# Finer waits for the gated products and the second feed-forward product of a fused adaLN and ternary feed-forward kernel

## Chip, core and metric

The kernel runs on one core of a Trainium2 chip. The metric is the time of one execution on the device, in microseconds (us). Before the change the median of 3 runs is 344.57 us (344.53 to 345.72). Differences of some 0.5% are about the smallest that can be told from no change here.

## What is computed

32 sequences of 32 tokens with 256 features go through a conditioned transformer layer and then through a gated feed-forward layer with ternary weights; the sum with the input is the result.

```python
def cond(x, timestep_embed, ...):                 # first layer
    shift1, scale1, gate1, shift2, scale2, gate2 = split(timestep_embed @ ada_w + ada_b, 6)
    x1 = ln(x) * (1 + scale1) + shift1
    q, k, v = (x1 @ qkv_w + qkv_b)                # 16 heads of 128
    a = softmax(q @ k.T * 128 ** -0.5) @ v        # inside each sequence of 32
    x = x + gate1 * (a @ out_w + out_b)
    x2 = ln(x) * (1 + scale2) + shift2
    h = gelu(x2 @ ffn_w1 + ffn_b1)                # 1024 wide
    return x + gate2 * (h @ ffn_w2 + ffn_b2)

def ffn(x, w1, g1, w2, g2, w3, g3):               # second layer, ternary weights, inputs quantised to int8
    swish = silu(linear_bit(x, w1, g1))           # 1024 wide
    h = swish * linear_bit(x, w2, g2)
    return linear_bit(h, w3, g3)

out = x + ffn(cond(x, cond_2048))
```

## The kernel before

Every engine's program is written out by hand as one list, and semaphores alone order the engines. The 1024 tokens are four quarters of 256 (`Q`, `b` or `a` in the code), and a quarter is two tiles `t` of 128 tokens. The 16 heads are four groups of four. A unit `u` is one group of heads over one quarter; there are 16 units. The products in float32 are made in three passes (`three_pass`): every operand is split into a high part and a low part, and high by high, high by low and low by high are added up in one bank of PSUM.

Units 0 to 7 do two groups of heads for all quarters. Then the loop over `q` (0 to 3) does the other two groups, two units for each `q`, and weaves in the feed-forward work that is ready: for quarter `b = q - 1` the first and second product of the first layer's feed-forward (`ffn1`, `ffn2`), for quarter `a = q - 2` the second layer. Behind the loop stands an ending, written out in one piece, with the rest of quarters 2 and 3. The change touches two kinds of work on TensorE (PE).

**The gated products** (`z_product`). For tile `t` and half `c` of the 1024 hidden columns, four matmuls of 128x512 are made: two (k = 0, 1) with w1 into bank 0 of a pair of banks, then two with w2 into bank 1. ScalarE (ACT) reads bank 0 and makes the swish (`silu`, semaphore `silu_done`). Then VectorE (DVE) reads bank 1 and the swish and multiplies them (`hidden`, semaphore `h_ready`). In the loop all four products of a quarter, (t, c) = (0,0), (0,1), (1,0), (1,1), use one pair, `wide_bank`, so each of the last three waits until `hidden` of the one before it has read bank 1. PE has other work between them: an output projection ahead of (0,1), and one head's query and key projection (`qk_unit`, two groups of six matmuls of 128x256) ahead of (1,0) and of (1,1). A further such head, the transposes `x2_turn` and another head follow, and then the value projection `v_unit`, which waits for `qk_kept`, ACT's copies of queries and keys. ACT's list has here: `silu` (1,1), the load of the exponential's table, the exponential, and only then those copies. The loop does this for quarters 0 and 1 (q = 2 and 3). In the ending, `end_z(0)` to `end_z(7)` do quarters 2 and 3 over three pairs of banks in turn, and from `end_z(3)` on a pair comes round again.

**The second product** (`ffn2`). ACT makes the hidden activations in four chunks of two tiles (`gelu`), and rounds each chunk to its high part `h_hi` (`h_high`, semaphore `h_hi_made`). GpSimd (POOL), or DVE for some, makes the low part `h_lo`. The first call of a quarter, `ffn2(b, 0)`, waits for all four high chunks. Its 24 matmuls are 8 with high by high, 8 with the weight's low part by `h_hi`, and 8 with `h_lo`, before which it waits for the low parts. It is called for quarters 0, 1 and 2; quarter 3 has its own form, `end_ffn2`, which the change leaves alone.

Of the kernel before, what the change touches and what calls it, by code (L numbers as in the profile page):

```python
# [60 lines left out]
def adaln_bitffn(nc, x, cond, ada_w, ada_b, qkv_w, qkv_b, out_w, out_b, ffn_w1, ffn_b1, ffn_w2, ffn_b2,  # L61
# [12 lines left out]
    MT = MLP // P  # L74
# [3 lines left out]
    NQ = T // QT  # L78
# [7 lines left out]
    NU = 2 * HALF  # L86
# [27 lines left out]
    with ExitStack() as ctx:  # L114
# [3 lines left out]
        def sem(name):  # L118
            return ctx.enter_context(nc.semaphore(name))
# [133 lines left out]
        proj_bank, att_bank, wide_bank = [[pair[:, i, :] for i in range(2)] for pair in (proj_banks, att_banks, wide_banks)]  # L253
# [17 lines left out]
        end_z_banks = [(proj_bank, att_bank, wide_bank)[i % 3] for i in range(len(END_Z))]  # L271
# [72 lines left out]
        at_lo_made = sem("at_lo_made")  # L344
# [16 lines left out]
        gelu_done = sem("gelu_done")  # L361
        h_hi_made = sem("h_hi_made")
        h_lo_made = sem("h_lo_made")
        h_lo_dve = sem("h_lo_dve")
        ffn2_mm = sem("ffn2_mm")
# [14 lines left out]
        silu_done = sem("silu_done")  # L380
        h_ready = sem("h_ready")
# [15 lines left out]
        out_ready = sem("out_ready")  # L397
# [147 lines left out]

        @block.tensor
        def _(pe):
            def three_pass(dst, pairs, start=True, stop=True, late=None):
                hi = [(a, c) for a, b, c, d in pairs]
                left_lo = [(b, c) for a, b, c, d in pairs]  # L550
                right_lo = [(a, d) for a, b, c, d in pairs]
                seq = hi + (left_lo + right_lo if late is not None and late[0] == "rhs" else right_lo + left_lo)
                for i, (l, r) in enumerate(seq):
                    if late is not None and i == 2 * len(pairs):
                        for made, n in late[1:]:
                            pe.wait_ge(made, n)
                    mm = pe.matmul(dst, l, r, start=start and i == 0, stop=stop and i == len(seq) - 1)  # L557
                return mm

            def qk_unit(u, h, late=None):  # L560
                g, Q, c, r = group(u), quarter(u), h // (HG // HALVES), h % (HG // HALVES)
                hi, lo = w_hi[g % 2], w_lo[g % 2]
                if r == 0:
                    pe.wait_ge(qk_hi, HALVES * g + c + 1)
                    pe.wait_ge(qk_lo, HALVES * g + c + 1)
                if h >= 2:
                    pe.wait_ge(qk_kept, 2 * HG * u + 2 * (h - 1))
                elif u > 0 and h == 0:
                    pe.wait_ge(shifted, u)
                elif u > 0:  # L570
                    pe.wait_ge(v_kept, 2 * u)
                for s in range(2):
                    cols = [slice(c * CH + (s * KD + k) * HW + r * P, c * CH + (s * KD + k) * HW + (r + 1) * P)
                            for k in range(KD)]
                    mm = three_pass(proj_bank[h % 2][:, s * QT:(s + 1) * QT],
                                    [(hi[:, cols[k]], lo[:, cols[k]], x1_hi[:, Q, k, :], x1_lo[:, Q, k, :])
                                     for k in range(KD)], late=late if s == 0 else None)
                mm.then_inc(projected, 1)
# [21 lines left out]
            def v_unit(u, t):  # L600
                g, Q = group(u), quarter(u)
                if t == 0:
                    pe.wait_ge(vw_hi, g + 1)
                    pe.wait_ge(vw_lo, g + 1)
                pe.wait_ge(qk_kept, 2 * HG * u + 2 * HG - 2 + 2 * t)
                tok = slice(t * P, (t + 1) * P)
                cols = [slice(SLOT + k * GC, SLOT + (k + 1) * GC) for k in range(KD)]
                three_pass(proj_bank[t][:, :],
                           [(x1_hi[:, Q, k, tok], x1_lo[:, Q, k, tok], w_hi[g % 2][:, cols[k]], w_lo[g % 2][:, cols[k]])
                            for k in range(KD)]).then_inc(projected, 1)  # L610
# [43 lines left out]
            def out_proj(u, t):  # L654
                g, Q, j = group(u), quarter(u), u % 2
                if t == 0:
                    pe.wait_ge(wo_hi_made, g + 1)
                    pe.wait_ge(wo_lo_made, g + 1)
                    if j == 0 and 0 < u <= HALF:
                        pe.wait_ge(acc_kept, u // 2)  # L660
                    elif j == 0 and u > HALF:
                        pe.wait_ge(out_read, Q)
                pe.wait_ge(at_hi_made, 2 * u + 2)
                three_pass(out_bank[:, t * D:(t + 1) * D],
                           [(at_hi[:, t, h, :], at_lo[:, t, h, :], wo_hi[g % 2][:, h, :], wo_lo[g % 2][:, h, :])
                            for h in range(HG)], start=(j == 0 and t == 0), stop=(j == 1 and t == 1),
                           late=("lhsT", (at_lo_made, 2 * u + 2)) if t == 0 else None).then_inc(out_mm, 1)
# [97 lines left out]
            def ffn2(b, t):  # L765
                if t == 0:
                    pe.wait_ge(f2_lo_made, 2)
                    pe.wait_ge(x2_scaled, b + 1)
                    pe.wait_ge(h_hi_made, (MT // 2) * (b + 1))
                    if b >= 1:  # L770
                        pe.wait_ge(hq_kept, 2 * b if b == NQ - 2 else 2 * b - 1)
                tok = slice(t * P, (t + 1) * P)
                lows = ((h_lo_made, (MT // 2) * (b + 1) - 2), (h_lo_dve, 2)) if b == NQ - 2 else (
                    (h_lo_made, (MT // 2) * (b + 1)),)
                three_pass(turn_bank[:, t * D:(t + 1) * D],
                           [(h_hi[:, m, tok], h_lo[:, m, tok], f2_hi[:, m, :], f2_lo[:, m, :])
                            for m in range(MT)],
                           late=("lhsT", *lows) if t == 0 else None).then_inc(ffn2_mm, 1)

            def end_ffn2(b, j):  # L780
                last = MT // 2 - 1
# [27 lines left out]
                                          rounded(xg[:, t, i, k * P:(k + 1) * P]), ident_h[:, :])  # L809
                mm.then_inc(q_turned, 1)  # L810

            def z_product(b, t, c, banks=wide_bank):
                if c == 0:
                    pe.wait_ge(q_kept, 2 * b + t + 1)
                if b < NQ - 2 and 2 * t + c > 0:
                    pe.wait_ge(h_ready, 4 * b + 2 * t + c)
                for i in range(2):
                    for k in range(KD):
                        mm = pe.matmul(banks[i][:, :], qt_bf[:, b, t, i * KD + k, :], w12t[:, i, k, c * MC:(c + 1) * MC],  # L819
                                       start=(k == 0), stop=(k == KD - 1))  # L820
                mm.then_inc(z_mm, 1)

            def end_z(i):
                b, t, c = END_Z[i]
                earlier = [j for j in range(i) if end_z_banks[j] is end_z_banks[i]]
                if earlier:
                    pe.wait_ge(h_ready, 4 * (NQ - 2) + earlier[-1] + 1)
                elif end_z_banks[i] is wide_bank:
                    pe.wait_ge(out_ready, 2 * (NQ - 2))
                elif end_z_banks[i] is att_bank:  # L830
                    pe.wait_ge(gelu_done, MT * NQ)
                else:
                    pe.wait_ge(at_lo_made, 2 * NU)
                z_product(b, t, c, end_z_banks[i])

            def hq_turn(b, t, rows, bank=turn_bank):
                pe.wait_ge(hq_rounded, 2 * b + t + 1)
# [75 lines left out]
            for q in range(NQ):  # L913
                u, b, a = HALF + 2 * q, q - 1, q - 2
# [10 lines left out]
                if a >= 0:  # L925
                    pe.wait_ge(at_lo_made, 2 * u)
                    z_product(a, 0, 0)
                    q_turn(a, 1)
                    score(u)
                out_proj(u - 1, 1)  # L930
                if a >= 0:
                    z_product(a, 0, 1)
# [17 lines left out]
                if u < NU - 1:  # L950
                    if b >= 0:
                        pe.wait_ge(at_lo_made, 2 * u)
                        ffn1(b, range(MT))
                    if a >= 0:
                        hq_turn(a, 0, h_tiles[0])
                    out_proj(u - 1, 1)
                    if a >= 0:
                        last_of_pair(a, b, 0)
                        hq_turn(a, 1, h_tiles[1], att_bank[0])
                    if b >= 0:  # L960
                        ffn2(b, 0)
                    if a >= 0:
                        last_of_pair(a, b, 1)
                    if b >= 0:
                        ffn2(b, 1)
# [3 lines left out]
            a, b = NQ - 2, NQ - 1  # L969
# [13 lines left out]
            for t in range(2):  # L983
                end_x2_turn(b, t)
            ffn2(a, 0)
            ffn2(a, 1)
            ffn1(b, range(MT), end_ffn1_bank, True)
# [1128 lines left out]
```

## Time and profile before

| | |
|---|---|
| median of 3 runs | 344.57 us |
| the profiled execution | 345.1 us |
| its span, first to last instruction | 343.3 us |
| PE busy | 333.1 us, 97% of the span |
| VectorE busy | 214.4 us, 62% |
| ScalarE busy | 182.3 us, 53% |
| GpSimd busy | 122.5 us, 36% |
| TensorE clock granted | 1.00 of full speed throughout |

The profile is one execution. The 1.8 us between its time and its span lie outside the instructions. The ends of matmuls are modelled, so two matmul rows overlap on the page, and the distance from one start to the next is what a matmul costs. An idle time in brackets counts from that modelled end. A row "x8" is a run of eight alike instructions with the start of the first.

### The profile page before, as it was taken

Reading aid. Unit: us, or ns where it says so; the run is one execution under the profiler, and the core shown is the slowest. Engines: PE = TensorE matmul, PEld = TensorE weight load, DVE = VectorE, ACT = ScalarE, POOL = GpSimd, SP = SyncE. Lnnn points to the kernel's source line nnn. Section 1 sums busy time; section 2 is a strip of 40 time slices with the busy share of each in tenths; the row PEclk is TensorE's granted clock in tenths of the full one; section 3 lists DMA queues with packets and bytes.
Section 4 is the critical chain, followed back from the end, with each engine's and each line's share of the span. In section 5 each row is a group of like instructions: output and inputs, shape, how many; then the busy total and the mean of one; then the engine's idle time right before and its main releaser. Section 6 shows DMA issues by size and latency. Waiting matters only on the chain. (4 is left out here: it accounts for less than half of the span.)

```text
span 343.3 us, 9835 instructions
## 1 busy us (share of the span) xinstructions
PE 333.1 (97%) x4205; PEld 301.2 (88%) x4205; DVE 214.4 (62%) x420; ACT 182.3 (53%) x352; POOL 122.5 (36%) x112
## 2 busy tenths in 40 slices
PE   8999999999999999999999999999999999999886
PEld 8889989899998989989898998789998789997665
DVE  3647966825859942513376064689375599865886
ACT  2654554455424565356334535478263667437684
POOL 2364405001923861656020630225330233113681
DMA  7974930500063540210020000200010200100001
GB/s 243 365 266 150 316 130 0 154 2 2 2 205 106 179 149 13 63 32 2 2 64 4 1 32 0 63 3 2 26 37 2 63 3 2 64 31 2 0 2 61
DMA packets 20834, 24.41 MB, mean 71 GB/s; under 512 B 1780, under 2 KB 18328, under 8 KB 20792
## 3 DMA queue, kind: packets, MB, share of 16 engines
q1 hardware_dynamic: 20416, 23.50, 21.1%
q8 instruction: 33, 0.54, 0.6%
q10 hardware_dynamic: 376, 0.30, 0.3%
q14 instruction: 9, 0.07, 0.1%
HBM read 22.68 MB, written 1.11 MB: 69 GB/s over the span
## 5 line engine op out<-in xcount | busy, mean ns | idle before, releaser
L1605 ACT ACTIVATE q_t<-proj_banks,bias_cols 128x256 f32<-128x256 f32 x64 | 30.5, 477 | 55.5 <-PE proj_banks L557 55.5
L557 PE MATMUL proj_banks<-x_hi,w_hi 128*128 128x256 f32 x252 | 52.8, 291 | 0.0
L557 PE MATMUL proj_banks<-x_lo,w_hi 128*128 128x256 f32 x252 | 50.7, 283 | 0.0
L557 PE MATMUL proj_banks<-x_hi,w_lo 128*128 128x256 f32 x252 | 50.7, 283 | 0.0
L1198 DVE TENSOR_TENSOR v_sb<-proj_banks,bv_row 128x512 f32<-128x512 f32 x32 | 21.7, 685 | 31.5 <-PE wide_banks L650 30.0
L557 PEld LDWEIGHTS proj_banks<-x_hi,w_hi 128*128 128x128 f32 x252 | 39.6, 191 | 1.5 <-issue 0.6
L557 PEld LDWEIGHTS proj_banks<-x_hi,w_lo 128*128 128x128 f32 x252 | 39.2, 191 | 0.0
L557 PEld LDWEIGHTS proj_banks<-x_lo,w_hi 128*128 128x128 f32 x252 | 39.2, 191 | 0.0
L650 PEld LDWEIGHTS att_banks<-probs_t,v_sb 32*128 32x128 f32 x512 | 29.8, 186 | 5.5 <-issue 5.4
L650 PE MATMUL att_banks<-probs_t,v_sb 32*128 32x32 f32 x512 | 31.6, 272 | 0.0
L1605 ACT ACTIVATE k_t<-proj_banks,bias_cols 128x256 f32<-128x256 f32 x64 | 30.2, 471 | 0.0
L650 PE MATMUL wide_banks<-probs_t,v_sb 32*128 32x32 f32 x480 | 29.6, 272 | 0.0
L650 PEld LDWEIGHTS wide_banks<-probs_t,v_sb 32*128 32x128 f32 x480 | 27.9, 186 | 0.0
L1614 ACT CAST at_hi<-att_banks 128x512 fp32r<-128x512 f32 x16 | 9.4, 588 | 33.0 <-PE wide_banks L650 32.6
L2000 POOL TENSOR_TENSOR h_lo<-work,h_hi 128x512 fp32r<-128x512 f32 x10 | 15.1, 1523 | 21.3 <-ACT h_hi L1692 21.0
L557 PE MATMUL proj_banks<-w_hi,x_hi 128*128 128x512 f32 x64 | 22.1, 427 | 0.4 <-ACT k_t L1605 0.4
L1941 POOL TENSOR_TENSOR w_lo<-stage,w_hi 128x1024 fp32r<-128x1024 f32 x6 | 15.2, 2547 | 18.6 <-DVE w_hi L1153 15.0
L557 PE MATMUL out_bank<-wo_hi,at_hi 128*128 128x256 f32 x128 | 21.8, 292 | 0.0
L557 PE MATMUL out_bank<-wo_hi,at_lo 128*128 128x256 f32 x128 | 20.3, 280 | 0.0
L557 PE MATMUL out_bank<-wo_lo,at_hi 128*128 128x256 f32 x128 | 20.3, 280 | 0.0
L557 PE MATMUL proj_banks<-w_lo,x_hi 128*128 128x512 f32 x64 | 20.0, 393 | 0.0
L557 PE MATMUL proj_banks<-w_hi,x_lo 128*128 128x512 f32 x64 | 19.9, 392 | 0.0
(299 smaller groups left out, 774.3 us busy)
## 6 DMA issues: line engine op xcount, KB each, us to landing
stage<-in_L_cond_qkv_w SPq DMA_DIRECT2D x16, 256.0 KB, 4.5
gate<-gate_rows_scratch SPq DMA_DIRECT2D x48, 64.0 KB, 2.4
stage<-in_L_cond_qkv_w SPq DMA_DIRECT2D x4, 512.0 KB, 5.3
stage<-in_L_cond_out_w SPq DMA_DIRECT2D x4, 512.0 KB, 4.4
work<-in_L_ffn_w SPq DMA_DIRECT2D x2, 1024.0 KB, 9.7
xin<-in_x SPq DMA_DIRECT2D x7, 256.0 KB, 2.9
bv_row<-in_L_cond_qkv_b SPq DMA_DIRECT2D x4, 256.0 KB, 5.0
work<-in_L_cond_ada_w SPq DMA_DIRECT2D x1, 1024.0 KB, 10.3
```

The costliest lines, as they stand in the source:

```text
L557: mm = pe.matmul(dst, l, r, start=start and i == 0, stop=stop and i == len(seq) - 1)
L650: mm = pe.matmul(dst, v_sb[r, t, h * P:(h + 1) * P], probs_t[r, t * HG + h, :], start=True, stop=True)
L1198: dve.tensor_tensor(v_sb[:, t, :], proj_bank[t][:, :], bv_row[:, u % 2, :], ALU.add).then_inc(v_kept, 1)
L1605: act.activation(dst[:, h, :], proj_bank[h % 2][:, s * QT:(s + 1) * QT], ACT.Identity, bias=bias_cols[:, c:c + 1]).then_inc(qk_kept, 1)
L1614: act.copy(att_to(at_hi, p), att_from(u, p)).then_inc(at_hi_made, 1)
L1941: pool.tensor_tensor(w_lo[g % 2][:, s], stage[:, s], w_hi[g % 2][:, s].bitcast(F32), ALU.subtract).then_inc(qk_lo, 1)
L2000: pool.tensor_tensor(h_lo[:, m, :], hf(2 * j, 2), h_hi[:, m, :].bitcast(F32), ALU.subtract).then_inc(h_lo_made, 1)
```

## The change

`z_product` now waits for two things at two places. Ahead of its two matmuls into bank 0 it waits for the swish of the product that used the pair before (`silu_done`), and ahead of the two into bank 1 for that product's gating (`h_ready`). Before, one wait for `h_ready` stood ahead of all four. `end_z` passes the number on instead of waiting itself, for the products from the fourth on. `ffn2(b, 0)` waits for the high parts chunk by chunk: one chunk ahead of each pair of its first eight matmuls, instead of all four chunks ahead of the first.

```diff
-            def three_pass(dst, pairs, start=True, stop=True, late=None):
+            def three_pass(dst, pairs, start=True, stop=True, late=None, each=None):
...
                 for i, (l, r) in enumerate(seq):
+                    if each is not None and i < len(pairs) and i % 2 == 0:
+                        pe.wait_ge(each[0], each[1] + i // 2 + 1)
...
                     pe.wait_ge(x2_scaled, b + 1)
-                    pe.wait_ge(h_hi_made, (MT // 2) * (b + 1))
...
-                           late=("lhsT", *lows) if t == 0 else None).then_inc(ffn2_mm, 1)
+                           late=("lhsT", *lows) if t == 0 else None,
+                           each=(h_hi_made, (MT // 2) * b) if t == 0 else None).then_inc(ffn2_mm, 1)
...
-            def z_product(b, t, c, banks=wide_bank):
+
+            def z_product(b, t, c, banks=wide_bank, held=None):
                 if c == 0:
                     pe.wait_ge(q_kept, 2 * b + t + 1)
                 if b < NQ - 2 and 2 * t + c > 0:
-                    pe.wait_ge(h_ready, 4 * b + 2 * t + c)
+                    held = 4 * b + 2 * t + c
                 for i in range(2):
+                    if held is not None:
+                        pe.wait_ge((silu_done, h_ready)[i], held)
...
-                if earlier:
-                    pe.wait_ge(h_ready, 4 * (NQ - 2) + earlier[-1] + 1)
-                elif end_z_banks[i] is wide_bank:
-                    pe.wait_ge(out_ready, 2 * (NQ - 2))
-                elif end_z_banks[i] is att_bank:
-                    pe.wait_ge(gelu_done, MT * NQ)
-                else:
-                    pe.wait_ge(at_lo_made, 2 * NU)
-                z_product(b, t, c, end_z_banks[i])
+                held = 4 * (NQ - 2) + earlier[-1] + 1 if earlier else None
+                if not earlier:
...
+                z_product(b, t, c, end_z_banks[i], held)
```

PE's list at product (1,0) of a quarter in the loop, before; its rows name the bank's pair, the operands and, in brackets, the semaphores waited for:

```order
L557 MATMUL proj_banks<-x_hi,w_lo_62 128x256 x2
L819 MATMUL wide_banks<-w12t,qt_bf 128x512 [waits h_ready,q_kept]
L819 MATMUL wide_banks<-w12t,qt_bf 128x512 x3
L557 MATMUL proj_banks<-x_hi,w_hi_60 128x256 [waits v_kept]
L557 MATMUL proj_banks<-x_hi,w_hi_60 128x256
```

The wait for `h_ready` held all four matmuls, and the next head's projection behind them. PE's list at the same place after:

```order
L559 MATMUL proj_banks<-x_hi,w_lo_62 128x256 x2
L824 MATMUL wide_banks<-w12t,qt_bf 128x512 [waits silu_done,q_kept]
L824 MATMUL wide_banks<-w12t,qt_bf 128x512
L824 MATMUL wide_banks<-w12t,qt_bf 128x512 [waits h_ready]
L824 MATMUL wide_banks<-w12t,qt_bf 128x512
L559 MATMUL proj_banks<-x_hi,w_hi_60 128x256 [waits v_kept]
L559 MATMUL proj_banks<-x_hi,w_hi_60 128x256
```

The wait for `h_ready` now stands two matmuls later; the matmuls and their order are the same. PE's list at `ffn2(0, 0)`, before, with the end of an output projection ahead of it:

```order
L557 MATMUL out_bank<-wo_hi_63,at_lo 128x256 x4
L557 MATMUL turn_bank<-f_hi,h_hi 128x256 [waits h_hi_made,x2_scaled,f2_lo_made]
L557 MATMUL turn_bank<-f_hi,h_hi 128x256 x7
L557 MATMUL turn_bank<-f_lo,h_hi 128x256 x8
L557 MATMUL turn_bank<-f_hi,h_lo 128x256 [waits h_lo_made]
L557 MATMUL turn_bank<-f_hi,h_lo 128x256 x7
```

One wait for all four chunks stood at its head. The same place after:

```order
L559 MATMUL out_bank<-wo_hi_63,at_lo 128x256 x4
L559 MATMUL turn_bank<-f_hi,h_hi 128x256 [waits h_hi_made,x2_scaled,f2_lo_made]
L559 MATMUL turn_bank<-f_hi,h_hi 128x256
L559 MATMUL turn_bank<-f_hi,h_hi 128x256 [waits h_hi_made]
L559 MATMUL turn_bank<-f_hi,h_hi 128x256
...
L559 MATMUL turn_bank<-f_lo,h_hi 128x256 x8
L559 MATMUL turn_bank<-f_hi,h_lo 128x256 [waits h_lo_made]
```

The row with its own wait and the one behind it stand there three times, once for each further chunk, so the wait for the last chunk moved behind six matmuls. No other engine's list changes.

## Rows read from the trace of the kernel before

**Rows 1.** The page, first part: engine, busy us, share of the span, instructions

```profile
PE 333.1 (97%) x4205; PEld 301.2 (88%) x4205; DVE 214.4 (62%) x420; ACT 182.3 (53%) x352; POOL 122.5 (36%) x112
```

**Rows 2.** Waits of PE, longest first: total us, times, longest us

```profile
PE wide_banks L819 <- DVE work L1363: 0.7, 2, 0.4
...
PE wide_banks L819 <- DVE h_odd L1363: 0.5, 2, 0.3
```

**Rows 3.** Timeline (start us, us long, engine), PE, products (1,0) and (1,1), quarter 0

```profile
217.80 0.40 PE L557 MATMUL proj_banks<-x_hi,w_lo 128*128 128x256 f32 x2
218.58 1.02 PE L819 MATMUL wide_banks<-w12t,qt_bf 128*128 128x512 fp8e4 x4 [0.38 <-DVE work L1363]
219.25 0.59 PE L557 MATMUL proj_banks<-x_hi,w_hi 128*128 128x256 f32 x2
...
220.63 0.40 PE L557 MATMUL proj_banks<-x_hi,w_lo 128*128 128x256 f32 x2
221.29 1.04 PE L819 MATMUL wide_banks<-w12t,qt_bf 128*128 128x512 fp8e4 x4 [0.26 <-DVE h_odd L1363]
```

**Rows 4.** Timeline of ACT (swishes) and of DVE (gatings) around these products

```profile
216.88 0.69 ACT L1719 ACTIVATE work<-wide_banks,deq 128x512 f32<-128x512 f32 x1 [2.24 <-PE wide_banks L819]
...
219.69 0.69 ACT L1719 ACTIVATE work<-wide_banks,deq 128x512 f32<-128x512 f32 x1 [0.61 <-issue]
...
217.68 0.75 DVE L1363 SCALAR_TENSOR_TENSOR work<-wide_banks,deq,work 128x512 f32<-128x512 f32 x1 [0.27 <-ACT work L1719]
...
220.48 0.75 DVE L1363 SCALAR_TENSOR_TENSOR h_odd<-wide_banks,deq,work 128x512 f32<-128x512 f32 x1 [1.17 <-ACT work L1719]
```

**Rows 5.** Timeline: PE's product (0,0) of quarter 0, which finds its banks free

```profile
212.33 1.04 PE L819 MATMUL wide_banks<-w12t,qt_bf 128*128 128x512 fp8e4 x4
213.20 0.39 PE L808 MATMUL turn_bank<-ident_h,work 128*128 128x128 f16 x4
```

**Rows 6.** Timeline: ACT's last copy ahead of the value projection, and that projection

```profile
225.19 0.46 ACT L1605 ACTIVATE k_t<-proj_banks,bias_cols 128x256 f32<-128x256 f32 x1
...
225.79 0.70 PE L557 MATMUL proj_banks<-w_hi,x_hi 128*128 128x512 f32 x2 [0.18 <-ACT k_t L1605]
```

**Rows 7.** Timeline of PE, ACT and POOL at `ffn2(0, 0)`

```profile
193.21 0.63 PE L557 MATMUL out_bank<-wo_hi,at_lo 128*128 128x256 f32 x4
194.22 1.19 PE L557 MATMUL turn_bank<-f_hi,h_hi 128*128 128x256 f32 x8 [0.38 <-ACT h_hi L1692]
...
196.20 1.12 PE L557 MATMUL turn_bank<-f_hi,h_lo 128*128 128x256 f32 x8
...
193.46 0.62 ACT L1692 CAST h_hi<-work 128x512 fp32r<-128x512 f32 x1
...
194.15 1.29 POOL L2000 TENSOR_TENSOR h_lo<-work,h_hi 128x512 fp32r<-128x512 f32 x1
```

**Rows 8.** Timeline at `ffn2(2, 0)`, and at four like transposes of quarter 0

```profile
223.59 0.60 PE L734 MATMUL turn_bank<-ident,xt 128*128 128x128 f32 x4
223.95 0.48 PE L557 MATMUL proj_banks<-x_hi,w_hi 128*128 128x256 f32 x2
...
297.40 0.60 PE L742 MATMUL att_banks<-ident,xt 128*128 128x128 f32 x4
298.00 1.18 PE L557 MATMUL turn_bank<-f_hi,h_hi 128*128 128x256 f32 x8
...
297.12 0.62 ACT L1692 CAST h_hi<-work 128x512 fp32r<-128x512 f32 x1
```

**Rows 9.** Timeline: PE at the head of `ffn1`'s seventh tile, which has a wait

```profile
237.34 0.40 PE L557 MATMUL wide_banks<-x_hi,f_lo 128*128 128x256 f32 x2
237.58 0.40 PE L557 MATMUL wide_banks<-x_hi,f_hi 128*128 128x256 f32 x2
```

**Rows 10.** Timeline: the last gated product (`end_z(7)`), and ACT's seventh swish

```profile
328.51 1.04 PE L819 MATMUL att_banks<-w12t,qt_bf 128*128 128x512 fp8e4 x4
...
329.39 0.68 ACT L1729 ACTIVATE late_swish<-proj_banks,deq 128x512 f32<-128x512 f32 x1
```

More of the change, by code:

```diff
@@ L825, in end_z @@
                 earlier = [j for j in range(i) if end_z_banks[j] is end_z_banks[i]]
-                if earlier:
-                    pe.wait_ge(h_ready, 4 * (NQ - 2) + earlier[-1] + 1)
-                elif end_z_banks[i] is wide_bank:
-                    pe.wait_ge(out_ready, 2 * (NQ - 2))
-                elif end_z_banks[i] is att_bank:
-                    pe.wait_ge(gelu_done, MT * NQ)
-                else:
-                    pe.wait_ge(at_lo_made, 2 * NU)
-                z_product(b, t, c, end_z_banks[i])
+                held = 4 * (NQ - 2) + earlier[-1] + 1 if earlier else None
+                if not earlier:
+                    if end_z_banks[i] is wide_bank:
+                        pe.wait_ge(out_ready, 2 * (NQ - 2))
+                    elif end_z_banks[i] is att_bank:
+                        pe.wait_ge(gelu_done, MT * NQ)
+                    else:
+                        pe.wait_ge(at_lo_made, 2 * NU)
+                z_product(b, t, c, end_z_banks[i], held)
             def hq_turn(b, t, rows, bank=turn_bank):
```

## The prediction

> **What bounds the kernel now.** I read the busy times of the page first. PE is busy for 333.1 us, 97% of the span, and VectorE, the next, for 62% [rows 1]. So until the ending, time comes only from PE's idle gaps, and an edit that removes no matmul, like this one, can give back at most the gaps it touches. The second view is the list of PE's waits. In the loop it names DVE's gating as releaser of the gated products four times, 0.7 us in two and 0.5 us in two [rows 2]. Six products have the changed wait there, three for each of two quarters, so two of them, (0,1) of each quarter, show no gap. The third view is the timeline around these gaps and around the three calls of `ffn2(b, 0)`. Idle times in brackets count from a modelled end; I work from starts instead: a row's start plus its number of matmuls times their cost is when PE could have gone on.
>
> **Costs used.** A gated product of four matmuls takes 213.20 - 212.33 = 0.87 us [rows 5], so a pair takes 0.43. Two matmuls of 128x256 take 237.58 - 237.34 = 0.24 us [rows 9].
>
> **Product (1,0).** PE is ready at 217.80 + 0.24 = 218.04 and starts at 218.58 [rows 3], 0.54 late. The swish that reads bank 0 ends at 216.88 + 0.69 = 217.57 [rows 4], before PE is ready, so the pair into bank 0 can start at 218.04 and is done at 218.47. The gating that reads bank 1 ends at 217.68 + 0.75 = 218.43 [rows 4], and PE went on 0.15 behind that. So the pair into bank 1 starts at 218.58, as the whole product did, and ends at 219.01 instead of 219.44. Gain: 0.43 us, the pair that now lies inside the wait. DVE still ends last here; 0.11 us of the gap stays.
>
> **Product (1,1).** All that leads to it follows the first by 0.43 us. The next swish started at 219.69, that is 1.11 behind the start of the first product's matmuls and 0.25 behind the end of the last; it becomes 219.26. Its gating started 0.79 later and took 0.75 [rows 4]; it becomes 220.05 to 220.80. PE is ready at 220.63 + 0.24 - 0.43 = 220.44 and the swish ends at 219.95, so bank 0's pair runs from 220.44 to 220.87. Bank 1 is read by 220.80. Between that end and PE's start lay 221.29 - 221.23 = 0.06 here [rows 3, 4], so PE may go on at 220.86 and finds its queue ready at 220.87. The product ends at 221.30 instead of 221.29 + 0.87 = 222.16: 0.86 us in all. The margin is 0.01 us, but a miss costs only its own size.
>
> **What comes next, and whether it follows.** The next place at which PE stands is the value projection, at 225.79, behind ACT's copy that ends at 225.19 + 0.46 = 225.65 [rows 6]. If that copy kept its time, the gain would be lost. ACT's list ahead of it is the swish of (1,1), a table load, the exponential and the copies, without a pause, and that swish starts when product (1,1) ends. So the copy moves by the same 0.86 us. Gain of a quarter: 0.86 us. The same pair of gaps stands in quarter 1 (two waits in each of the two rows) [rows 2], and the neighbouring work is the same: 2 x 0.86 = 1.72 us.
>
> **`ffn2(0, 0)`.** PE is ready at 193.21 + 0.48 = 193.69 and starts at 194.22 [rows 7], 0.53 late, because the fourth high chunk ends at 193.46 + 0.62 = 194.08. The three chunks before it are long made. Six matmuls on them take 0.72 us, until 194.41, and by then (194.22) the fourth chunk may be read. So the gap goes entirely: 0.53 us. What is late next? The low parts: POOL's last one ends at 194.15 + 1.29 = 195.44, and PE used it at 196.20 [rows 7]. Now PE comes at 195.67. With 0.14 us from an engine's end to PE's start, as for the high chunk, that still holds, by 0.09 us.
>
> **`ffn2(1, 0)` and `ffn2(2, 0)`.** The first has no wait of PE behind `h_hi` in the list, so nothing. For the second, four transposes precede it at 297.40; four like ones took 223.95 - 223.59 = 0.36 [rows 8], so PE was ready at 297.76 and started at 298.00. The last chunk ended at 297.12 + 0.62 = 297.74 [rows 8]. Gain at most 0.24 us; at least zero, if the transposes themselves waited for their input and PE was ready later than that. I take 0.22, near the upper end, since the 0.60 us that these four span is what the like ones span.
>
> **The ending.** `end_z(3)` to `end_z(7)` get the finer wait. Only the last shows a gap for it. It could start about 0.1 us earlier than 328.51, but ACT's list decides there: the swish of `end_z(6)` only starts at 329.39 [rows 10], so the last swish has to queue behind it. Nothing.
>
> **Cost of the waits themselves.** The change adds 20 waits on PE: 6 in the loop's products, 5 in the ending's, 9 in `ffn2`. A wait whose semaphore is already up shows no cost: `ffn1`'s seventh tile has one, and its first pair starts 0.24 us after the pair before, as everywhere [rows 9]. I take zero. The upper bound is in the third rival. The Trainium skill (Perfetto Trace Analysis, Identifying Dependency Chains) says that an instruction that waits on several engines may get separate EventSemaphore instructions ahead of it. That speaks against product (1,0), whose head waits for ACT's copy and ACT's swish; no row of this trace shows a price for it, and with none the sum stays as it is.
>
> **Sum.** 1.72 + 0.53 + 0.22 = 2.47 us. Everything behind these places is fed by PE or by what PE releases, so the ending should move as one block. The profiled execution would go from 345.1 to 342.6 us. Its own time lies 0.5 us above the median, 344.57; against that the forecast is 344.57 - 2.47 = **342.1 us**, 0.7% faster.
>
> **Rivals.**
> *Part of the gain is absorbed.* Product (1,1) needs swish and gating to move with (1,0), and the value projection needs ACT's copies to move too. If ACT or DVE is held by something PE doesn't feed (POOL's norm for DVE's next step, say), (1,0) still gives 0.43 and (1,1) nothing lasting: 2 x 0.43 + 0.53 = 1.4 us, giving 343.2. Against it: ACT sat idle for 0.61 us ahead of the swish of (1,0) and DVE for 1.17 us ahead of its gating [rows 4].
> *The change does nothing.* A PE wait that goes away reappears wholly at the next place fed from another engine, the value projection [rows 6] or, for `ffn2`, POOL's low part [rows 7]: 344.5 us. Against it: I found each of those feeders to start from the very product that moved.
> *Slower.* A wait in the middle of a product keeps the next weight load from running ahead under the matmuls before it. If each such load were exposed, by about 0.24 us (as much as a pair of 128x256 matmuls), 20 waits would cost 4.8 us against 2.47 gained: 346.9. It decides from 2.47 / 20 = 0.12 us for each. Its place is between the bank 0 and bank 1 pairs. The Trainium skill (TensorE: Matmul & The Clock Gate, on the reorder window) says that PE's queue pulls weight loads ahead of matmuls in flight, which is what such a wait would forbid. Against it stand the 0.24 us at the satisfied wait [rows 9].
> *More than forecast.* If the small gap left at (1,0) closes as well, and work behind gets a kinder overlap between DVE and POOL, 3.0 us: 341.5.
>
> **How the numbers follow.** Forecast 0.64, part absorbed 0.18, nothing 0.08, slower 0.04, more 0.06. The forecast's own range is 341.8 to 342.7, that is 1.9 to 2.8 us gained. The range to hold 8 in 10 takes in most of the absorbed case: 341.5 to 343.3. About 0.5%, 1.7 us, is what a measurement of this kernel can tell from no change; that bound lies at 342.85. Faster by more: 0.64 + 0.06 + a little of the absorbed case = 0.73. Slower by more: 0.03. Within: 0.24.
>
> **What the profile after would show.** Product (1,0): its row splits in two, with bank 0's pair right behind the projection and 0.1 us of gap before bank 1's pair. Product (1,1): no gap. The list of PE's waits has lost `wide_banks <- DVE`, or nearly. `ffn2(0, 0)` starts without a gap and its low-part matmuls wait for nothing. The value projection still waits 0.18 us for ACT's copy. The distance from `ffn2(0, 0)`'s end to the start of `ffn2(2, 0)` is 1.7 us shorter. I am wrong if new waits stand at the value projection or at POOL's low part, if a pair's spacing at a new wait is over 0.24 us where the semaphore is up, or if the ending, from the last feed-forward product on, is longer than before.

## The result and the profile after

The kernel after takes 342.18 us (median of 5 runs, 341.83 to 342.30), the kernel before 344.53 us (median of 5). The ratio is 0.9925, with a 95% interval of 0.9913 to 0.9936: 0.75% faster, where 0.7% was forecast (342.1 us, range 341.5 to 343.3). A second set of runs of the kernel after, on another occasion, gave 341.78 us and a ratio of 0.9905 (0.9878 to 0.9932).

The page's first part after, to be read beside [rows 1]; the profiled execution takes 342.06 us and its span is 340.3 us:

```profile
PE 331.5 (97%) x4205; PEld 300.1 (88%) x4205; DVE 214.4 (63%) x420; ACT 182.2 (54%) x352; POOL 122.5 (36%) x112
```

The work is the same to the instruction. The whole list of PE's waits after:

```profile
PE out_bank L810 <- DVE work L1346: 1.2, 1, 1.2
PE att_banks L868 <- DVE probs_t L1079: 1.0, 1, 1.0
PE proj_banks L559 <- ACT k_t L1610: 0.6, 3, 0.3
PE turn_bank L1026 <- issue: 0.6, 1, 0.6
PE wide_banks L1026 <- ACT late_hw L1902: 0.6, 1, 0.6
PE proj_banks L589 <- DVE xt L1146: 0.5, 1, 0.5
PE out_bank L559 <- DVE h_lo L1544: 0.4, 1, 0.4
PE att_banks L858 <- ACT late_hqt L1748: 0.4, 1, 0.4
PE att_banks L824 <- ACT qt_bf L1715: 0.2, 1, 0.2
```

The rows of [rows 2], `wide_banks` behind DVE's gating, are gone, and so is a wait of `turn_bank` behind `h_hi`. Of the three waits for `k_t` two are those of the value projections; the third, 0.3 us, lies in the first 14 us of the program and is looked at below. PE's timeline after at products (1,0) and (1,1) of quarter 0 and at the value projection behind them, to be read beside [rows 3] and [rows 6]; the last line is ACT's copy ahead of that projection:

```profile
216.93 0.40 PE L559 MATMUL proj_banks<-x_hi,w_lo 128*128 128x256 f32 x2
217.17 1.05 PE L824 MATMUL wide_banks<-w12t,qt_bf 128*128 128x512 fp8e4 x4
217.87 0.59 PE L559 MATMUL proj_banks<-x_hi,w_hi 128*128 128x256 f32 x2
...
219.24 0.40 PE L559 MATMUL proj_banks<-x_hi,w_lo 128*128 128x256 f32 x2
219.49 1.04 PE L824 MATMUL wide_banks<-w12t,qt_bf 128*128 128x512 fp8e4 x4
...
223.99 0.70 PE L559 MATMUL proj_banks<-w_hi,x_hi 128*128 128x512 f32 x2 [0.18 <-ACT k_t L1610]
...
223.38 0.47 ACT L1610 ACTIVATE k_t<-proj_banks,bias_cols 128x256 f32<-128x256 f32 x1
```

The product starts 0.24 us behind the row before it, the cost of two matmuls, where it was 0.78 us (218.58 - 217.80). At (1,1) it is 0.25 us, where it was 0.66. Each is one row of four matmuls: there is no gap between the two banks' pairs either. The value projection has the same 0.18 us of idle time as before and starts 4.50 us behind product (1,1), as before: ACT's copies have moved with the product.

Here is what holds bank 1's pair now. PE's weight load for it and DVE's gating ahead of it, after:

```profile
217.61 0.11 PEld L824 LDWEIGHTS wide_banks<-w12t,qt_bf 128*128 128x128 bf16 x2 [0.33 <-DVE work L1368]
...
216.81 0.75 DVE L1368 SCALAR_TENSOR_TENSOR work<-wide_banks,deq,work 128x512 f32<-128x512 f32 x1 [0.27 <-ACT work L1724]
...
219.10 0.75 DVE L1368 SCALAR_TENSOR_TENSOR h_odd<-wide_banks,deq,work 128x512 f32<-128x512 f32 x1 [0.66 <-ACT work L1724]
```

The gating ends at 216.81 + 0.75 = 217.56, the weight load starts 0.05 us behind it, and bank 0's pair keeps PE at work until 217.17 + 0.43 = 217.60. So the wait for the gating now lies under bank 0's pair, and only the weight loads' row shows it.

PE at `ffn2(0, 0)` and at `ffn2(2, 0)` after, beside [rows 7] and [rows 8]; the last line is POOL's last low part for `ffn2(0, 0)`:

```profile
192.93 0.63 PE L559 MATMUL out_bank<-wo_hi,at_lo 128*128 128x256 f32 x4
193.40 1.12 PE L559 MATMUL turn_bank<-f_hi,h_hi 128*128 128x256 f32 x8
...
195.32 1.12 PE L559 MATMUL turn_bank<-f_hi,h_lo 128*128 128x256 f32 x8
...
294.68 0.60 PE L744 MATMUL att_banks<-ident,xt 128*128 128x128 f32 x4
295.05 0.71 PE L559 MATMUL turn_bank<-f_hi,h_hi 128*128 128x256 f32 x4
...
193.88 1.29 POOL L2005 TENSOR_TENSOR h_lo<-work,h_hi 128x512 fp32r<-128x512 f32 x1
```

The product starts 0.47 us behind the projection row (1.01 before) and 0.37 us behind the transposes (0.60 before). Its low part follows at 1.92 us, without the 0.06 us by which it was slower before (1.98).

**A measure that does not depend on the head of the program.** The first changed instruction comes some 193 us into the span. Ahead of it the kernels have the same instructions, and yet the output projection row ahead of `ffn2(0, 0)` starts at 193.21 us in the profile of before [rows 7] and at 192.93 after. Over the eight profiles here with the same instructions up to there it lies between 192.51 and 193.21. So two spans can differ by 0.7 us for a reason that no edit has. The difference arises in the first 14 us. PE's first product with the layer's input `xt`, before and then after, and in the profile of after a wait behind it:

```profile
10.03 1.99 PE L587 MATMUL proj_banks<-xt,stage 128*128 128x256 f32 x8 [0.52 <-DVE xt L1141]
```

```profile
9.42 1.99 PE L589 MATMUL proj_banks<-xt,stage 128*128 128x256 f32 x8 [0.53 <-DVE xt L1146]
...
13.13 0.47 PE L559 MATMUL proj_banks<-x_hi,w_hi 128*128 128x256 f32 x2 [0.29 <-ACT k_t L1610]
```

In the eight profiles this product starts between 9.40 and 10.05 us, and from its start to the output projection it is 183.09 to 183.18 us in seven of them. In the profile of after it is 183.51, and that one alone has the wait at 13.13 us. The second profile of after does not have it, so it is not an effect of the change. Below I take the distance from the start of that row to the start of the last product's row of matmuls. The last rows, before and then after:

```profile
339.54 1.04 PE L1043 MATMUL turn_bank<-w3t,late_hqt 128*128 128x256 fp8e4 x8
```

```profile
336.51 1.04 PE L1048 MATMUL turn_bank<-w3t,late_hqt 128*128 128x256 fp8e4 x8
```

Before: 339.54 - 193.21 = 146.33 us. After: 336.51 - 192.93 = 143.58 us, 2.75 less. The second profile of after gives 143.55: the two differ by 0.03 us.

### The profile page after: what moved, and what is told of

It reads as the page before. It is cut to its first block and busy times, and to the rows that moved or that the text cites. A ratio compares the mean times of both kernels' runs of the same rounds, so it can differ in the third digit from the quotient of the medians.

```text
span 340.3 us, 9835 instructions
## 1 busy us (share of the span) xinstructions
PE 331.5 (97%) x4205; PEld 300.1 (88%) x4205; DVE 214.4 (63%) x420; ACT 182.2 (54%) x352; POOL 122.5 (36%) x112
```

## Experiments

The ratios of the experiments are to runs of the kernel before on the same chip as each experiment (there were three chips), whose medians were 344.86 to 344.94 us. Two distances are read from each profile: `tail`, the one just defined, and `gated`, from the start of product (0,0) to the start of the value projection, for quarters 0 and 1.

| kernel | tail us | gated us | median us | ratio to before, 95% interval |
|---|---|---|---|---|
| before | 146.33 | 13.46, 13.45 | 344.53 | |
| after | 143.58 | 12.53, 12.53 | 342.18 | 0.9925 (0.9913 to 0.9936) |
| e1_chunks | 145.56 | 13.46, 13.45 | 343.69 | 0.9966 (0.9952 to 0.9979) |
| e2_split_loop | 144.49 | 12.54, 12.53 | 342.92 | 0.9952 (0.9938 to 0.9965) |
| e3_split_end | 146.25 | 13.46, 13.45 | 344.43 | 0.9983 (0.9961 to 1.0004) |
| e4_swap | 146.18 | 13.39, 13.38 | 344.44 | 0.9993 (0.9984 to 1.0003) |
| e5_one_wait | 143.58 | 12.54, 12.55 | 341.64 | 0.9900 (0.9886 to 0.9915) |
| e6_two_waits | 145.33 | 12.59, 12.52 | 346.07 | 1.0033 (1.0020 to 1.0046) |
| e8_separate | 143.83 | 12.68, 12.66 | 342.15 | 0.9916 (0.9902 to 0.9931) |
| e7_order | 143.02 | 12.38, 12.39 | 341.00 | 0.9884 (0.9867 to 0.9900) |
| e9_order_before | 145.13 | 12.99, 13.01 | 343.72 | 0.9967 (0.9948 to 0.9986) |
| e10_after | 143.55 | 12.54, 12.52 | 341.78 | 0.9905 (0.9878 to 0.9932) |

By their times, e3_split_end and e4_swap can't be told from the kernel before. What is said of them rests on the distances of one profile each.

### Each part alone

e1_chunks is the kernel before with the chunked wait of `ffn2(b, 0)` alone:

```diff
+                    if each is not None and i < len(pairs) and i % 2 == 0:
+                        pe.wait_ge(each[0], each[1] + i // 2 + 1)
...
-                    pe.wait_ge(h_hi_made, (MT // 2) * (b + 1))
```

> The kernel before with one part of the change alone: ffn2(b, 0) waits for the high parts chunk by chunk. Theory (the gaps add up, and what is gained is kept to the end): the gap at ffn2(0, 0) goes, 0.54 us, and 0.23 us at ffn2(2, 0), together 0.77 us; the time goes from 344.5 to 343.8 us, and the distance from ffn2(0, 0)'s start to the last matmul changes by 0.23 us alone. Rival (absorbed): the gain reappears as a longer wait for POOL's low part or at the value projection, and the distances behind grow by what was gained; 344.5 us.

```profile
192.83 0.63 PE L559 MATMUL out_bank<-wo_hi,at_lo 128*128 128x256 f32 x4
193.30 1.12 PE L559 MATMUL turn_bank<-f_hi,h_hi 128*128 128x256 f32 x8
...
296.49 0.60 PE L744 MATMUL att_banks<-ident,xt 128*128 128x128 f32 x4
```

These are PE's rows of e1_chunks. The product starts 0.47 us behind the projection (1.01 before), and `tail` is 146.33 - 145.56 = 0.77 us shorter. `gated` is what it was. The rival, that POOL's low part or the value projection takes the gain, has fallen.

e2_split_loop is the kernel before with the split wait for the six products in the loop alone:

```diff
-                if b < NQ - 2 and 2 * t + c > 0:
-                    pe.wait_ge(h_ready, 4 * b + 2 * t + c)
+                held = 4 * b + 2 * t + c if b < NQ - 2 and 2 * t + c > 0 else None
                 for i in range(2):
+                    if held is not None:
+                        pe.wait_ge((silu_done, h_ready)[i], held)
```

> The kernel before with the finer wait of the gated products in the loop alone (six products of quarters 0 and 1). Theory: product (1,0) starts 0.54 us earlier and (1,1) another 0.43 us, in each of two quarters, 1.9 us in all: 344.5 becomes 342.6 us, with the distance from product (0,0) to the next value projection 12.53 instead of 13.46 us in both quarters. The recorded prediction's own size for it was 1.72 us: 342.8. Rival (absorbed): (1,0) alone keeps its gain, 0.9 to 1.1 us: 343.5.

`gated` fell by 0.92 us in both quarters and `tail` by 1.84 us. The three matmul rows of e2_split_loop that matter, products (0,0), (1,0) and (1,1), with the value projection:

```profile
211.72 1.04 PE L820 MATMUL wide_banks<-w12t,qt_bf 128*128 128x512 fp8e4 x4
...
217.44 1.05 PE L820 MATMUL wide_banks<-w12t,qt_bf 128*128 128x512 fp8e4 x4
219.75 1.04 PE L820 MATMUL wide_banks<-w12t,qt_bf 128*128 128x512 fp8e4 x4
224.26 0.47 PE L557 MATMUL proj_banks<-w_hi,x_hi 128*128 128x512 f32 x1 [0.17 <-ACT k_t L1606]
```

From (0,0) to (1,0) it is 5.72 us (218.58 - 212.33 = 6.25 before), and from (1,0) to (1,1) 2.31 us (2.71 before). Both gains are kept; absorption would have shown as a `gated` near 12.9.

e3_split_end is the kernel before with the split for `end_z(3)` to `end_z(7)` alone:

```diff
+                held = 4 * (NQ - 2) + earlier[-1] + 1 if earlier else None
...
-                    pe.wait_ge(h_ready, 4 * (NQ - 2) + earlier[-1] + 1)
...
+                z_product(b, t, c, end_z_banks[i], held)
```

> The kernel before with the finer wait in end_z(3) to end_z(7) alone. Theory: no time from the bank 0 wait itself, since ACT's list decides the ending. The waits at the head of end_z(4) change their places, though: the one for ACT's copy is now the one carried by the matmul and no longer a separate wait instruction, and PE starts 0.06 instead of 0.14 us behind that copy. So 0.08 us off the ending, 344.45 us. Rival (a gap is a gap): the 0.12 us ahead of end_z(7) come off the end too, 0.2 us in all; or nothing changes at all.

PE's row of `end_z(4)` before, and then PE's and ACT's rows of e3_split_end in the ending:

```profile
325.79 1.02 PE L819 MATMUL att_banks<-w12t,qt_bf 128*128 128x512 fp8e4 x4 [0.30 <-ACT qt_bf L1710]
```

```profile
325.00 1.04 PE L824 MATMUL att_banks<-w12t,qt_bf 128*128 128x512 fp8e4 x4 [0.21 <-ACT qt_bf L1715]
...
327.60 1.03 PE L824 MATMUL att_banks<-w12t,qt_bf 128*128 128x512 fp8e4 x4
...
324.84 0.59 ACT L1715 ACTIVATE qt_bf<-turn_bank 128x512 bf16<-128x512 f16 x1
...
328.61 0.68 ACT L1734 ACTIVATE late_swish<-proj_banks,deq 128x512 f32<-128x512 f32 x1
```

`end_z(4)` at 325.00 starts 0.62 us behind the transposes ahead of it; it was 0.70. `end_z(7)` at 327.60 comes 2.60 us behind `end_z(4)`, where it was 2.72: its gap of 0.12 us has gone. But ACT's swish of `end_z(6)` starts 1.01 us behind `end_z(7)`'s start, and no longer 0.88 (329.39 - 328.51, [rows 10]). From `end_z(4)` to that swish it is 3.61 us, and it was 3.60. The 0.12 us are given back there. Of the ending 0.08 us remain in `tail`, as was expected; the rival with 0.2 us has fallen.

The three parts give 0.77 + 1.84 + 0.08 = 2.69 us of the 2.75 that the whole change takes off `tail`. They add up.

### Why product (1,0) gave more than was forecast

Product (1,0) gave 0.54 us and not 0.43: its first pair started 0.54 us earlier, as forecast, but the 0.11 us of gap that were to stay ahead of its second pair are not there. Before, PE went on 0.15 us behind the gating's end at (1,0) and 0.06 behind it at (1,1). In the built program, an instruction that waits for several semaphores carries the wait that is written first. The further ones stand in separate wait instructions ahead of it, up to two waits in each. At (1,0) before, `q_kept` is written first, so `h_ready` is the separate one. At (1,1) there is only one wait, and in the kernel after bank 1's pair has only one as well. e4_swap changes nothing but the order of two lines in the kernel before:

```diff
-                if c == 0:
-                    pe.wait_ge(q_kept, 2 * b + t + 1)
                 if b < NQ - 2 and 2 * t + c > 0:
                     pe.wait_ge(h_ready, 4 * b + 2 * t + c)
+                if c == 0:
+                    pe.wait_ge(q_kept, 2 * b + t + 1)
```

> The kernel before with two lines in z_product swapped: the wait for h_ready is written ahead of the wait for q_kept. In the built program the first written wait is carried by the matmul, and every further one is a wait instruction of its own ahead of it. Theory (a separate wait instruction that is still open holds PE some 0.09 us longer than a carried one): product (1,0) starts 0.06 instead of 0.15 us behind the end of the gating that it waits for, in both quarters, as (1,1) does already; 0.2 us in all with the ending's end_z(4) and end_z(6) the other way round, 344.4 us. Rival (the 0.15 us belong to the place or to what the gating writes, not to the form of the wait): the start stays 0.15 us behind.

```profile
217.99 1.04 PE L819 MATMUL wide_banks<-w12t,qt_bf 128*128 128x512 fp8e4 x4 [0.29 <-DVE work L1363]
...
217.18 0.75 DVE L1363 SCALAR_TENSOR_TENSOR work<-wide_banks,deq,work 128x512 f32<-128x512 f32 x1 [0.27 <-ACT work L1719]
```

In e4_swap the gating ends at 217.93 and PE starts 0.06 us later. PE's idle time fell from 0.38 to 0.29 us, and 0.07 of these 0.09 us show in `gated`, in both quarters. The form of the wait makes the difference. (Nothing changed in the ending, where the expectation had named two products: their lines already stood in that order. So `tail` is 0.15 us shorter and not 0.2.)

e8_separate does the reverse to the kernel after:

```diff
+                    if held is not None and i == 1:
+                        pe.wait_ge(ident_made, 2)
                     if held is not None:
                         pe.wait_ge((silu_done, h_ready)[i], held)
```

> The kernel after, with a wait for a long raised semaphore written ahead of the wait for h_ready at bank 1's pair, so that the wait for h_ready becomes the separate instruction. Theory (form of the wait): at product (1,0) bank 1's pair starts 0.15 us behind the gating's end and no longer 0.04 behind it, 0.11 us later, and at (1,1) about 0.08 us later, which gives back 0.19 us of the 0.93 us gained in each of two quarters: the distance from product (0,0) to the value projection is 12.7 us instead of 12.53. The recorded prediction took the 0.15 us as given at (1,0). Rival (the form of the wait does nothing once the pair before it keeps PE at work): 12.53 us still.

```profile
217.90 0.13 PEld L826 LDWEIGHTS wide_banks<-w12t,qt_bf 128*128 128x128 bf16 x2 [0.39 <-issue]
...
217.03 0.75 DVE L1370 SCALAR_TENSOR_TENSOR work<-wide_banks,deq,work 128x512 f32<-128x512 f32 x1 [0.27 <-ACT work L1726]
```

In e8_separate the weight load starts 217.90 - 217.78 = 0.12 us behind the gating's end, against 0.05 after, and `gated` is 12.68 and 12.66 us, where 12.7 was expected and 12.53 by the rival. The split on these terms gives 0.78 and 0.79 us a quarter. That is a little under the 0.86 that was forecast, because here the wait at (1,1) is a separate one too. The weight loads' row names the releaser where the open wait is the carried one (DVE, after) and says "issue" here, where it is the separate one.

The Trainium skill (Perfetto Trace Analysis, Identifying Dependency Chains) says that an instruction that waits on several engines may have EventSemaphore instructions put ahead of it. These runs agree and put a price on it: 0.07 to 0.09 us for each hand-over on the path whose releasing wait is the separate one.

### What a wait costs whose semaphore is up

e5_one_wait and e6_two_waits are the kernel after with one and with two waits for long raised semaphores ahead of nearly every matmul of the three-pass products. The edit of e6_two_waits; e5_one_wait has the first of the two waits alone:

```diff
+                    if i > 0:
+                        pe.wait_ge(ident_made, 2)
+                        pe.wait_ge(filler_made, 1)
                     mm = pe.matmul(dst, l, r, start=start and i == 0, stop=stop and i == len(seq) - 1)
```

> The kernel after, with one more wait ahead of every matmul of a three-pass product but its first: for a semaphore that was raised at the very start. Nearly all of them are carried by their matmul: 1440 more matmuls carry a wait than in the kernel after, and 39 more separate wait instructions stand on PE. Theory (a wait whose semaphore is up costs nothing): 342.2 us, within 0.3 us, and pairs of 128x256 matmuls still 0.24 us apart. Rival (a wait keeps the next weight load from running ahead under the matmul before it): with the f32 load's 0.19 us exposed at most of them, 50 to 270 us more.

> The kernel after, with two such waits ahead of every matmul of a three-pass product but its first. The matmul carries one, the other becomes a wait instruction of its own: 1480 more of them on PE than in the kernel after. Theory: PE's front end works ahead of the matmuls, and a separate wait whose semaphore is up is passed before its matmul's turn; no time, 342.2 us within 0.5 us. Rival (each separate wait costs what one that is still open cost at product (1,0), 0.09 us, also when its semaphore is up): 1480 x 0.09 = 133 us more.

`ffn2(0, 0)` in e5_one_wait, and then in e6_two_waits, each row eight matmuls:

```profile
192.96 1.12 PE L561 MATMUL turn_bank<-f_hi,h_hi 128*128 128x256 f32 x8
193.91 1.12 PE L561 MATMUL turn_bank<-f_lo,h_hi 128*128 128x256 f32 x8
```

```profile
195.74 0.63 PE L562 MATMUL out_bank<-wo_hi,at_lo 128*128 128x256 f32 x4
196.21 1.18 PE L562 MATMUL turn_bank<-f_hi,h_hi 128*128 128x256 f32 x8
197.22 1.20 PE L562 MATMUL turn_bank<-f_lo,h_hi 128*128 128x256 f32 x8
198.26 1.20 PE L562 MATMUL turn_bank<-f_hi,h_lo 128*128 128x256 f32 x8
```

With 1440 more carried waits `tail` is 143.58 us, the same to the digit, and eight matmuls take 0.95 us. (The time of 341.64 us lies 0.56 below the 342.2 that were expected, more than the 0.3 allowed; the second set of the kernel after, 341.78 us, lies there too.) A carried wait that is already satisfied costs nothing, and the rival with exposed weight loads has fallen. The 20 waits that the change adds are all of this kind, and the number of separate ones is as before (179 on PE). With 1480 more separate waits `tail` is 1.75 us longer and the head of the program 2.8 us (195.74 against 192.93), 4.6 us in all or 3 ns each; the medians of the two runs, on the same chip, lie 4.43 us apart. In a dense row it is more: 1.01 and 1.04 us for eight matmuls against 0.96, up to 10 ns each. So neither theory held for separate waits. They aren't free, as mine said, and far from 0.09 us each. Whether the wait costs this or merely one more instruction in PE's list, no run separates.

### The order of the wait lines

e7_order is the kernel after, with the wait that comes last written first at eleven places on four engines. Three of them:

```diff
+                pe.wait_ge(qk_kept, 2 * HG * u + 2 * HG - 2 + 2 * t)
                 if t == 0:
                     pe.wait_ge(vw_hi, g + 1)
                     pe.wait_ge(vw_lo, g + 1)
-                pe.wait_ge(qk_kept, 2 * HG * u + 2 * HG - 2 + 2 * t)
...
-                act.wait_ge(deq_made, 2 * b + t + 1)
                 act.wait_ge(z_mm, n + 1)
+                act.wait_ge(deq_made, 2 * b + t + 1)
...
-                dve.wait_ge(deq_made, 2 * b + t + 1)
                 dve.wait_ge(silu_done, 4 * b + 2 * t + c + 1)
+                dve.wait_ge(deq_made, 2 * b + t + 1)
```

> The kernel after, with the order of wait lines changed and nothing else: where an instruction waits for several semaphores, the one that comes last by the trace is written first, so that the instruction carries it. Places: value projection and last products on PE, swishes and gelu on ACT, gatings and both residuals on DVE, root mean squares on POOL. Theory: 0.09 us off each such hand-over that lies on the path: the two value projections behind gated products (0.18 us), ACT's swish and DVE's gating where they still hold PE (little), and some five hand-overs of the ending (0.4 us): 0.6 us, 341.6 us. Rival (only PE pays for a separate wait): 0.2 us from the value projections and 0.1 us from the first last product, 341.9 us.

```profile
215.32 0.69 ACT L1725 ACTIVATE work<-wide_banks,deq 128x512 f32<-128x512 f32 x1 [2.23 <-PE wide_banks L824]
217.63 0.69 ACT L1725 ACTIVATE work<-wide_banks,deq 128x512 f32<-128x512 f32 x1
...
216.04 0.75 DVE L1369 SCALAR_TENSOR_TENSOR work<-wide_banks,deq,work 128x512 f32<-128x512 f32 x1 [0.19 <-ACT work L1725]
```

These are ACT's swishes and DVE's gating in e7_order. The gating starts 0.72 us behind the swish's start, where it was 0.81 in the kernel after (216.81 behind 216.00): DVE pays for a separate wait as PE does. In `gated` the 0.15 us all lie behind product (1,1), where the value projection starts 4.36 us later and no longer 4.50. The products themselves keep their distances, since the wait for the gating already lay under bank 0's pair. `tail` is 0.56 us shorter than after, 0.6 was expected, and the rival in which only PE pays had 0.3. The time is 341.00 us, ratio 0.9884 (0.9867 to 0.9900). This version beats both kernels: its interval lies below that of the kernel after, 0.9913 to 0.9936. It overlaps with that of the second set of after, 0.9878 to 0.9932, so the size of its lead is better taken from `tail`: 0.56 us, 0.16%. The runs on its own chip agree: e5_one_wait, whose added waits cost nothing, lies between 341.58 and 341.67 us, and e7_order between 340.91 and 341.19.

e9_order_before gives the same order to the kernel before, with `h_ready` ahead of `q_kept` and no split. e10_after is the kernel after once more, on the same chip as e9_order_before.

> The kernel before with the new order of wait lines of the run before, and h_ready ahead of q_kept at the gated products; no wait is split. Theory (each hand-over on the path gets 0.06 to 0.09 us shorter, on every engine): in each of two quarters (1,0) starts 0.09 us earlier, swish and gating between (1,0) and (1,1) 0.06 and 0.09, swish and value projection behind (1,1) 0.06 and 0.09, 0.39 us; with the 0.26 us of the ending 1.0 us off the 146.33 us from the output projection ahead of ffn2(0, 0) to the last matmul, and 343.5 to 343.9 us. The split of the waits on top of it (the kernel after with that order has 143.02 us there) would then be worth 2.3 us. Rival (the order helps only where the split has made room): 0.3 to 0.5 us off, 344.3 us.

> The kernel after, unchanged, on the same chip and against the same runs as the one with the new order without the split: 342.2 us, 143.58 us from the output projection ahead of ffn2(0, 0) to the last matmul, and up to 0.4 us of difference to its first profile in the stretch before that projection, in which the two kernels have the same instructions.

The order alone takes 1.20 us off `tail` (146.33 to 145.13) and 0.47 and 0.44 us off `gated`; 1.0 was expected. Without the split every hand-over from product to swish to gating to product lies on PE's path: from (0,1) to (1,0) it is 2.61 us in e9_order_before and 2.84 before, from (1,0) to (1,1) 2.60 and 2.71. So the order is worth more there (1.20 us) than with it (0.56). In the other direction, the whole change is worth 2.75 us with the old order and 145.13 - 143.02 = 2.11 us with the new one. The two share 0.6 us of the same gaps.

## Why the prediction was right, point by point

- **PE's gaps are the only source of time.** Right. PE's busy row has the same work, `tail` shrank by the gaps that went, and the parts added up.
- **Product (1,0), 0.43 us.** The mechanism was right, the size too small: 0.54 us. The step that failed is "So the pair into bank 1 starts at 218.58": it took PE's 0.15 us behind the gating's end as a property of the place. It belonged to a wait that was a separate instruction, and the change happened to turn it into a carried one (e4_swap, e8_separate). The weight load for bank 1's pair then starts 0.05 us behind the gating, just when bank 0's pair is done, and the 0.11 us of gap that were to stay are not there. The prediction had both figures in hand, 0.15 us at (1,0) and 0.06 at (1,1), and did not ask why they differ. That this came out in the kernel's favour was luck.
- **Product (1,1), another 0.43 us.** 0.39 us measured (2.71 to 2.32 us from one product to the next). The gap there was 221.29 - 220.87 = 0.42 us, so 0.43 was already 0.01 too much. The chain through swish and gating moved along as worked out, and the thin margin cost nothing.
- **The value projection follows.** Right: 4.50 us behind product (1,1) before and after. A quarter gave 0.93 us against 0.86.
- **`ffn2(0, 0)`, 0.53 us.** 0.54 us measured, and the low parts held, though only 0.09 us of room had been worked out for them. POOL's last one ends at 195.17 us in the profile after, 0.15 us ahead of the row that reads it, which starts on time (1.92 us behind the product's start, two rows of eight at 0.96).
- **`ffn2(1, 0)` nothing, `ffn2(2, 0)` 0.22 us.** Right: 0.43 us from transposes to product in both profiles for the first, and 0.23 us for the second.
- **The ending, nothing.** 0.08 us. The gap at `end_z(7)` closed and ACT's list gave it back, as argued. What I did not see is that the wait at `end_z(4)` changes its form.
- **The waits cost nothing.** Right for the kind that the change adds (e5_one_wait). The separate instructions that the Trainium skill speaks of (Perfetto Trace Analysis, Identifying Dependency Chains), and which the prediction set against product (1,0), number 179 on PE before and after: the change adds none. The prediction said that no row showed a price for them. The 0.15 us at (1,0) against the 0.06 at (1,1) were that price [rows 3, 4].
- **Sum.** 2.47 us forecast. `tail` shows 2.75: 2 x 0.93 + 0.54 + 0.23 + 0.08 = 2.71, and 0.05 us in the stretch between `ffn2(0, 0)` and product (0,0), from 18.11 to 18.06 us, which is the 0.06 us that `ffn2(0, 0)`'s own rows had lost behind the gap. Of the excess of 0.28 us, 0.14 are product (1,0) with (1,1) and 0.08 the ending, both by the form of the waits. The medians moved by 2.35 us and the ratio by 0.75%, 2.6 us. The profiled execution came out at 342.06 and not at 342.6 us: 0.28 us of that is this excess, and 0.28 us the one of before had lost more ahead of the first changed instruction.
- **The rivals.** Partial absorption is refuted by `gated` and by e2_split_loop, no effect by the result, and slower, with its exposed weight loads, by e5_one_wait. "More than forecast" came true in part: the small gap at (1,0) closed as well. A kinder overlap of DVE and POOL had no part in it that I can see.
- **The signs.** The list of PE's waits, `ffn2(0, 0)`, product (1,1) and the value projection's 0.18 us are as said. Product (1,0) shows no gap of 0.1 us. From the start of `ffn2(0, 0)`'s last eight matmuls to the start of `ffn2(2, 0)` it is 101.80 us before and 99.73 after, 2.07 us shorter and not 1.7. Of the difference 0.22 is the gain of `ffn2(2, 0)` itself, which the prediction left out of this distance though it had it in its sum.

What stays open: why PE's first product with `xt` starts between 9.40 and 10.05 us in profiles of the same instructions. No run here was made for it.

## What to carry to other kernels

If two readers empty two banks one after the other, let the producer wait for each bank's own reader: the second wait then passes under the work into the first bank, and up to one bank's matmuls come off every round. Write the wait that comes last as the first one at its instruction, so that the instruction itself carries it. And before summing such gains, look at what follows: they are kept where the next waiting engine is itself fed by the work that moved.

## What the runs showed of the hardware

- Through a wait that the matmul carries, PE's weight load started 0.05 us behind the end of DVE's instruction and the matmul 0.06; through a separate wait instruction it was 0.12 and 0.15 us.
- DVE shows nearly the same difference behind ACT (0.79 to 0.81 us from start to start after, 0.72 in e7_order), and ACT behind PE shows 0.04 to 0.06 us (the swish of (1,0) starts 1.14 us behind the product after, and 1.08 us in e7_order).
- A satisfied carried wait cost PE nothing in 1440 cases (e5_one_wait). A satisfied separate one cost 3 ns on average and up to 10 ns in a dense row of matmuls (e6_two_waits).
